# Grams of two steps in a row, then the value products of two steps in a row, in the similarity loop of a metaformer block

## The chip, the cores and the metric

The kernel runs on 1 core of one Trainium2 chip. The metric is the device time of one execution in microseconds (us); lower is better.

## What is computed

The input is x with 32 images of 64 channels and 48 x 48 pixels (P = 2304 pixels). Two blocks follow each other; the change lies in the first.

```
def _L0_conv_ref(x, Wc, bc):            # GAMMA = 2, EPS = 1e-08
    xf = x.reshape(B, C, P)
    nrm = jnp.maximum(jnp.sqrt(jnp.sum(xf * xf, axis=1)), EPS)
    xn = xf / nrm[:, None, :]
    s = jax.nn.relu(jnp.einsum('bcp,bcq->bpq', xn, xn)) ** GAMMA
    g = jnp.einsum('oc,bcp->bop', Wc, xf) + bc[None, :, None]
    out = jnp.einsum('bpq,bcq->bcp', s, g)
...
x = x + _L0_conv_ref(_ln_c(x), L0_conv_Wc, L0_conv_bc)
t = _to_tokens(x)
t = t + _L0_ffn_ref(_ln_t(t), ...)
```

So each image (the kernel calls it a batch b) needs a matrix of cosines of all 2304 x 2304 pairs of its pixels (the gram), its relu squared, and the product of that with g (the values). `_L0_ffn_ref` is a mixture of four experts whose gates come from attention over a graph of 262,144 edges between tokens.

## The kernel before, in words

The engines run programs of their own, written out by hand, and meet at semaphores. The span has four stages: images 0 to 7 together with the sorting of the edges (to about 1400 us); images 8 to 31, which is the loop of this study, from 1408 to 3683 us, while GpSimd gathers rows of the graph one after the other; the segments of the graph (to about 4350 us); the experts.

In the loop an image has STEPS = 45 steps t. The pixels of the output are cut in five chunks `CH` (four of 512 columns, one of 256, here called wide and narrow), and for each chunk the other pixels are taken in PAIRS = 9 pairs of 128 rows, so t = 9 x chunk + pair. For a step:

- PE makes a gram: for each of two row groups one matmul of high by high and low parts and one that adds the rest, both in f16 (lines 1874 and 1875), into the tile `gram[(par + t) % 2]`. There are two such tiles, used in turn; `par` changes with each image and 45 is odd, so the turns go on across images.
- ACT makes `rel`, the scaled relu of the gram (line 2064). In every third step (t % 3 == 0) ACT also squares it into `s2` (line 2068).
- In the other steps DVE multiplies the gram by `rel` into `s2` (line 2404). It reads the gram tile too, so the tile is free only after it.
- PE multiplies `s2` with the values `gT` into `acc` (function `values`, line 1830, two f32 products in the two halves of the columns, four matmul records in the trace), three steps late (LAG = 3). In the last narrow steps, and in the three first of the next image, these matmuls have 256 columns.

A gram waits for the last reader of its tile, two steps back, by one of these:

```
if t % 3 == 2:
    pe.wait_ge(a_rel, STEPS * own + (t - 1))
else:
    at_least(pe, v_s2, by_dve(STEPS) * own + by_dve(t - 1))
```

Between the steps stands work for the image before and the image after. On PE, after the values of the steps named: `post` (steps 5, 7, 9), `tokens` (15, 17), `pre` (19, 21, 23), `turn` (33, 35). On ACT, after the relu (and square) of the steps: `post` (6, 8, 10), `deviation2` (12), `tokens` (16, 18), `pre` (20, 22, 24), `deviation`, `norm`, `high` (26, 28, 30), `turned` (34, 36: copies into `hl`, line 1987). On DVE, after its product: `sums` of a finished chunk (3, 12, 21, 30, 39), norms, `value_rows` (28: `vr` line 2360 and `gT` line 2362), `units` (29), `low` (31) and, for the first sixteen of the loop's images, `level` (a piece of the graph's sorting). The function `walk` runs the body for the first image, twice in each turn of two program loops, and for the last image. After the last image SP lifts `img_done`, for which GpSimd waits before the next stage.

Of the kernel before, what the change touches and what calls it, by code (L numbers as in the profile page):

```python
# [22 lines left out]
P = 128  # L23
# [11 lines left out]
def chunks(n, size=512):  # L35
    return [(o, min(size, n - o)) for o in range(0, n, size)]
# [1201 lines left out]
def flow(nc, n, Wc, bc, Wg, att_s, att_d, b_gat, gamma, beta, W1, b1, W2, b2):  # L1238
# [5 lines left out]
    CH = chunks(NP)  # L1244
    NCH = len(CH)
    PAIRS = QT // 2
    STEPS = NCH * PAIRS
# [45 lines left out]
    with ExitStack() as ctx, ExitStack() as early, ExitStack() as late:  # L1293
# [3 lines left out]
        def sem(name):  # L1297
            return ctx.enter_context(nc.semaphore(name))

        def im_sb(name, shape, dt=F32):  # L1300
            return early.enter_context(nc.sbuf_tensor(name, shape, dt))

        def im_pb(name, shape):
            return early.enter_context(nc.psum_tensor(name, shape, F32))

        def ph(name, shape, dt=F32):
            return late.enter_context(nc.sbuf_tensor(name, shape, dt))
# [27 lines left out]
        hl = im_sb("hl", [P, 2, NP], F16)  # L1335
        lh = im_sb("lh", [P, 2, NP], F16)
# [8 lines left out]
        gram = [im_pb(f"gram{i}", [P, 2, 512]) for i in range(2)]  # L1345
# [6 lines left out]
        own = ph("own", [P, 2, TW, RW])  # L1352
# [70 lines left out]
        pe_gram = sem("pe_gram")  # L1423
        a_rel = sem("a_rel")
        a_s2 = sem("a_s2")
        v_s2 = sem("v_s2")
# [86 lines left out]
        def by_dve(k):  # L1513

            return k - (k + 2) // 3
# [5 lines left out]
        def at_least(eng, semaphore, value):  # L1521

            if not isinstance(value, int) or value > 0:
                eng.wait_ge(semaphore, value)
# [240 lines left out]
        def _(pe):  # L1765
            n.merge_tensor(pe)
            def pre(b, par, i):

                if i == 0:
                    at_least(pe, n.a_tn, NB * (b - 1))  # L1770
                else:
                    pe.wait_ge(n.a_cv, NB * b + i)
                s0, k = BATCH[i]
                for s in range(s0, s0 + k):
                    for h in range(2):
                        rows = slice(h * C, (h + 1) * C)
                        last = pe.matmul(misc[:, h, (s - s0) * P:(s - s0 + 1) * P], xh[rows, par, s * P:(s + 1) * P], n.wpre[rows, :],  # L1777
                                         start=True, stop=True)
                last.then_inc(n.pe_pre, 1)

            def turn(b, i):

                q0, k = TBATCH[i]
                if i == 0:
                    pe.wait_ge(n.v_lo, b + 1)
                if i >= 2:
                    pe.wait_ge(n.a_hl, NTB * b + i - 1)
                bank = misc[:, i % 2, :].bitcast(F16)
                for q in range(q0, q0 + k):
                    last = pe.transpose(bank[:, (q - q0) * P:(q - q0 + 1) * P], tw[:, q, :, :].rearrange("p a c -> p (a c)"), n.ident16[:, :])  # L1790
                last.then_inc(n.pe_tr, 1)

            def post(b, par, i):

                if i == 0:
                    pe.wait_ge(n.v_x2, NCH * (b + 1))
                    at_least(pe, n.a_tn, NB * b)
                else:
                    pe.wait_ge(n.a_c2, NB * b + i)
                s0, k = BATCH[i]  # L1800
                for s in range(s0, s0 + k):
                    for h in range(2):
                        rows = slice(h * C, (h + 1) * C)
                        last = pe.matmul(misc[:, h, (s - s0) * PW:(s - s0 + 1) * PW], x2[rows, par, s * P:(s + 1) * P], n.wpost[rows, :],  # L1804
                                         start=True, stop=True)
                last.then_inc(n.pe_post, 1)

            def tokens(b, i):

                if i == 0:  # L1810
                    pe.wait_ge(n.v_t2, b + 1)
                if i >= 2:
                    pe.wait_ge(n.a_tn, NB * b + i - 1)
                s0, k = BATCH[i]
                for s in range(s0, s0 + k):
                    last = pe.transpose(misc[:, i % 2, (s - s0) * P:(s - s0 + 1) * P], t2[:, s, :, :].rearrange("p a c -> p (a c)"), n.ident[:, :])
                last.then_inc(n.pe_tt, 1)

            def values(b, own, par, u):

                c, k = divmod(u, PAIRS)
                w = CH[c][1]
                pe.wait_ge(v_s2, by_dve(STEPS) * own + by_dve(u + 1))
                pe.wait_ge(a_s2, by_act(STEPS) * own + by_act(u + 1))
                if k == 0:
                    at_least(pe, n.v_x2, NCH * b + c - 1)
                    if c == 0:
                        pe.wait_ge(n.v_g, b + 1)
                for j in (0, 1):
                    last = pe.matmul(acc[(par + c) % 2][j * C:(j + 1) * C, 0:w], gT[:, par, 2 * k + j, :], s2[:, u % SLOTS, j * w:(j + 1) * w],  # L1830
                                     start=k == 0, stop=k == PAIRS - 1)
                if k == PAIRS - 1:
                    last.then_inc(n.pe_acc, 1)

            used = 0
            for turn_no, kind in enumerate(ROUTES):
# [3 lines left out]
                for q in range(banks_of(kind)):  # L1840
                    if used >= 3:
                        pe.wait_ge(a_route, used - 2)
                    bank = routed_ps[0:rows_out, used % 3, :].rearrange("p (j c) -> p j c", c=rows_in)
                    used += 1
                    for k in range(min(per, count - q * per)):
                        j = q * per + k
# [4 lines left out]
                        last = pe.transpose(bank[:, k, :], part, n.ident[:, :])  # L1851
# [7 lines left out]
                        turn(FIRST, i)  # L1859
            pe.wait_ge(a_route, routes_done[-1])  # L1860

            def body(b, own, par, nth, before, more, moved=None):
                pe.wait_ge(n.l_in[par], 32 * (nth + 1))
                for t in range(STEPS):
                    c, k = divmod(t, PAIRS)
                    o, w = CH[c]
                    if t % 3 == 2:
                        pe.wait_ge(a_rel, STEPS * own + (t - 1))
                    else:
                        at_least(pe, v_s2, by_dve(STEPS) * own + by_dve(t - 1))  # L1870
                    bank = gram[(par + t) % 2]
                    for j in (0, 1):
                        pixels = slice((2 * k + j) * P, (2 * k + j + 1) * P)
                        pe.matmul(bank[:, j, 0:w], hl[:, par, pixels], hl[:, par, o:o + w], start=True, stop=False)  # L1874
                        last = pe.matmul(bank[:, j, 0:w], lh[:, par, pixels], hl[:, par, o:o + w], start=False, stop=True)  # L1875
                    last.then_inc(pe_gram, 1)
                    if t >= LAG:
                        values(b, own, par, t - LAG)
                    elif before:
                        values(b - 1, own - 1, 1 - par, STEPS + t - LAG)  # L1880
                    if before and t in POST_PE:
                        post(b - 1, 1 - par, POST_PE[t])
                    if before and t == 15:
                        tokens(b - 1, 0)
                        tokens(b - 1, 1)
                    if before and t == 17:
                        tokens(b - 1, 2)
                    if more and t in PRE_PE:
                        if t == 19:
                            pe.wait_ge(n.x_in[1 - par], 64 * (nth + 1 + par))  # L1890
                        pre(b + 1, 1 - par, PRE_PE[t])
                    if more and t == 33:
                        turn(b + 1, 0)
                        turn(b + 1, 1)
                    if more and t == 35:
                        turn(b + 1, 2)
            walk(pe, body)
            for t in range(LAG):
                values(B - 1, NI - 1, 1, STEPS + t - LAG)
# [9 lines left out]
            for k in range(3):  # L1909
                for q in range(G):  # L1910
                    last = pe.transpose(turn_ps[:, k, q * P:(q + 1) * P], tails[:, k, q, :], n.ident[:, :])  # L1911
                last.then_inc(pe_tails, 1)
            pe.wait_ge(v_car, 1)
            for k, t in enumerate((So, Mo)):
                for q in range(G):
                    last = pe.transpose(back_ps[:, k, q, :], t[:, q * P:(q + 1) * P], n.ident[0:NC5, 0:NC5])
# [764 lines left out]
```

## Time and profile before

| | us |
|---|---|
| median of 3 runs | 5337.25 (5335.33 to 5337.66) |
| span of the profiled execution, first to last instruction | 5332.3 |
| PE busy (matmul) | 3735.5 (70%) |
| DVE busy | 3969.2 (74%) |
| ACT busy | 3397.9 (64%) |
| POOL busy | 2944.3 (55%) |

The profiled execution's own time isn't listed beside its span; the span lies 3.0 us under the fastest run and 4.9 under the median. PE is TensorE's matmul row, DVE VectorE, ACT ScalarE, POOL GpSimd, SP SyncE. In a timeline row stand the start, the duration, the engine, the line, the operation, output and inputs, the shape and how many were merged; in brackets the idle time of the engine before it and what ended it. The end of a matmul is modelled, and starts 0.22 us apart with durations of 0.38 are matmuls that follow each other without a gap. PEclk is the share of TensorE's full clock that was granted.

### The profile page before, as it was taken

How to read it: one execution, taken by the hardware profiler on the slowest of the kernel's cores; microseconds unless marked ns; L12 is line 12 of the kernel's file. 1: busy time of each engine (PE TensorE's matmuls, PEld its weight loads, DVE VectorE, ACT ScalarE, POOL GpSimd, SP SyncE). 2: the span in 40 equal slices, each digit the busy share in tenths (PEclk: the TensorE clock that was granted, in tenths of full speed). 3: DMA queues.
4: the chain of work that ended last, by engine and by line, in shares of the span. 5: the costliest groups of instructions: out<-in, count | busy, mean ns of one | idle time of the engine just before them, and what ended most of it. 6: DMA issues, size and time to landing. Idle time of an engine off the chain costs nothing.

```text
span 5332.3 us, 61957 instructions
## 1 busy us (share of the span) xinstructions
PE 3735.5 (70%) x18367; PEld 1259.1 (24%) x18367; DVE 3969.2 (74%) x5512; ACT 3397.9 (64%) x4285; POOL 2944.3 (55%) x2937
## 2 busy tenths in 40 slices
PE   4888988400599999999999999996000017787888
PEld 1223333200233333333333333332000002222222
DVE  8998988997666666666666654554999947787877
ACT  4777988401676767676676776775566536666665
POOL 6000000058777777777777777774666147666661
PEclk9899999755799999999999999998555558888889
DMA  6100100002112122222212222223555526999997
GB/s 259 33 20 25 29 20 17 15 14 82 28 41 58 40 61 48 47 58 46 62 42 52 52 46 56 42 46 87 189 184 186 184 75 137 150 160 162 158 161 141
DMA packets 332447, 441.38 MB, mean 83 GB/s; under 512 B 183193, under 2 KB 261916, under 8 KB 331500
## 3 DMA queue, kind: packets, MB, share of 16 engines
q1 hardware_dynamic: 209744, 288.12, 19.8%
q0 software_dynamic: 105536, 148.61, 16.0%
q10 hardware_dynamic: 16896, 1.18, 0.2%
q8 instruction: 152, 2.49, 0.2%
q14 instruction: 119, 0.97, 0.1%
HBM read 252.35 MB, written 166.47 MB: 79 GB/s over the span
## 4 chain that ended last, share of the span: by engine, by line
PE 36%; DVE 26%; issue 6%; ACT 5%; DMA 5%; POOL 1%; SPq 1%; DVEq 0%; ACTq 0%; POOLq 0%
PE acc L1830 13%; PE gram L1874 8%; PE gram L1875 6%; DVE s L2404 3%; DMA gs<-gates_d 3%; PE ye L1928 2%; PE up L1940 2%; ACT rel L2064 2%; DVE S L2503 2%; DVE AD L2488 2%; DVE AE L2482 2%; DVE ms L2623 1%; POOL R L1761 1%; PE misc L1804 1%; PE misc L1777 1%
## 5 line engine op out<-in xcount | busy, mean ns | idle before, releaser
L980 POOL DMA_INDIRECT rows<-htab_d,idx x2048 | 2141.5, 1046 | 730.7 <-issue 599.0
L2404 DVE SCALAR_TENSOR_TENSOR s<-gram,rel 128x1024 f32<-128x1024 f32 (+1 forms) x720 | 802.6, 1117 | 849.2 <-ACT rel L2064 844.1
L2064 ACT ACTIVATE rel<-gram 128x1024 f32<-128x1024 f32 (+1 forms) x1080 | 1009.5, 940 | 605.4 <-PE gram L1875 570.4
L1830 PE MATMUL acc<-s,gT 128*64 128x512 f32 (+1 forms) x4320 | 1076.6, 577 | 0.0
L1874 PE MATMUL gram<-hl 128*128 128x512 f16 (+1 forms) x2160 | 776.7, 365 | 117.3 <-DVE s L2404 95.9
L1875 PE MATMUL gram<-hl,lh 128*128 128x512 f16 (+1 forms) x2160 | 765.8, 360 | 0.0
L1761 POOL DMA_INDIRECT R<-seg_d,nidx x576 | 584.5, 1015 | 191.2 <-issue 165.9
L1928 PE MATMUL ye<-hid,w 128*64 128x384 f32 x1536 | 381.4, 577 | 250.8 <-DVE ms L2623 188.5
L1080 POOL IOTA slots<- 64x2048 int32 x1 | 1.8, 1832 | 974.4 <-POOLq L192 974.4
L2156 ACT ACTIVATE hid<-up,b1t 128x768 f32<-128x768 f32 x384 | 333.2, 899 | 259.6 <-PE up L1940 258.4
L1911 PE MATMUL tailsT<-ident,tails 128*20 128x128 f32 x24 | 4.7, 385 | 599.6 <-DVE tails L2511 599.6
L1874 PEld LDWEIGHTS gram<-hl 128*128 128x128 f16 x2160 | 211.0, 98 | 854.0 <-DVE s L2404 387.7
L906 ACT ACTIVATE w_s2r<-w_gram 128x1024 f32<-128x1024 f32 (+1 forms) x360 | 348.6, 968 | 93.2 <-PE w_gram L775 92.7
L316 DVE TENSOR_TENSOR edges<-edges 128x2048 f32<-128x2048 f32 (+1 forms) x186 | 370.7, 1993 | 46.9 <-ACT edges L935 41.2
L1940 PE MATMUL up<-tne,w 64*128 64x384 f32 x1536 | 403.0, 606 | 0.8 <-DVEq L2525 0.6
L317 DVE TENSOR_TENSOR edges<-edges 128x2048 f32<-128x2048 f32 (+1 forms) x186 | 369.7, 1987 | 0.0
L749 PE MATMUL w_acc<-w_s2r,w_gT 128*64 128x512 f32 (+1 forms) x1440 | 364.0, 585 | 0.6 <-ACT w_s2r L888 0.6
L888 ACT ACTIVATE w_s2r<-w_s2r 128x1024 f32<-128x1024 f32 (+1 forms) x360 | 361.5, 1004 | 0.0
L2068 ACT ACTIVATE s<-rel 128x1024 f32<-128x1024 f32 (+1 forms) x360 | 349.7, 971 | 11.4
L2623 DVE SCALAR_TENSOR_TENSOR ms<-ye,b2c,gs 128x384 f32<-128x384 f32 x384 | 232.2, 616 | 148.8 <-PE up L1940 100.9
L1830 PEld LDWEIGHTS acc<-s,gT 128*64 128x64 f32 x4320 | 214.5, 135 | 414.2 <-issue 400.8
L774 PE MATMUL w_gram<-w_hl 128*128 128x512 f16 (+1 forms) x720 | 264.6, 373 | 44.6 <-DVEq L491 13.3
(372 smaller groups left out, 5351.0 us busy)
## 6 DMA issues: line engine op xcount, KB each, us to landing
gs<-gates_d SPq DMA_DIRECT2D x64, 1024.0 KB
rows<-htab_d,idx POOLq DMA_INDIRECT x2048
seg_d<-state SPq DMA_DIRECT2D x32, 996.0 KB, 4.8
raw_d<-w_zeros POOLq DMA_DIRECT2D x48, 512.0 KB, 23.3
raw_d<-rows POOLq DMA_DIRECT2D x32, 768.0 KB, 3.7
tne<-tn_d SPq DMA_DIRECT2D x32, 576.0 KB
x2e<-x_d SPq DMA_DIRECT2D x32, 576.0 KB
out<-res SPq DMA_DIRECT2D x64, 256.0 KB
```

What stands on the lines that cost most here:

```text
L316: dve.tensor_tensor(lo, a, b, ALU.min)
L317: step(dve.tensor_tensor(hi, a, b, ALU.max))
L749: last = pe.matmul(acc[(b + c) % 2][j * C:(j + 1) * C, 0:w], gT[:, b % 2, 2 * k + j, :], s2(s)[:, j * w:(j + 1) * w], start=k == 0, stop=k ...
L980: pool.indirect_dma_start(out=n.rows[:, k % 2, j, :], out_offset=None, in_=n.htabx, in_offset=bass.IndirectOffsetOnAxis(ap=n.idx[:, g % 2, ...
L1761: pool.indirect_dma_start(out=R[:, par, j, :], out_offset=None, in_=n.seg, in_offset=bass.IndirectOffsetOnAxis(ap=nidx[:, par, j:j + 1], a ...
L1830: last = pe.matmul(acc[(par + c) % 2][j * C:(j + 1) * C, 0:w], gT[:, par, 2 * k + j, :], s2[:, u % SLOTS, j * w:(j + 1) * w], start=k == 0 ...
L1874: pe.matmul(bank[:, j, 0:w], hl[:, par, pixels], hl[:, par, o:o + w], start=True, stop=False)
L1875: last = pe.matmul(bank[:, j, 0:w], lh[:, par, pixels], hl[:, par, o:o + w], start=False, stop=True)
L1928: last = pe.matmul(y[i % 2][h * C:(h + 1) * C, 0:EW], w2[:, k, :], hid[:, i % GROUP, h, :], start=True, stop=True)
L1940: last = pe.matmul(up[i % GROUP][:, h, 0:EW], w1[rows_, k, :], tne[rows_, par, cp * EW:(cp + 1) * EW], start=True, stop=True)
L2064: act.activation(rel[:, t % RELS, 0:2 * w].rearrange("p (j x) -> p j x", j=2), gram[(par + t) % 2][:, :, 0:w], ACT.Relu, scale=1.0 / SPLIT ...
L2404: dve.scalar_tensor_tensor(halves(s2[:, t % SLOTS, 0:2 * w]), gram[(par + t) % 2][:, :, 0:w], 1.0 / SPLIT ** 2, halves(rel[:, t % RELS, 0: ...
```

## The change

The code that makes a gram becomes a function `gram_of(own, par, t)`, unchanged inside, waits included. In the loop it is called for t and t + 1 when t is even, and the values follow as before, so PE runs gram t, gram t + 1, values t - 3, values t - 2. Step 44 stays single. Programs of ACT, DVE, POOL and SP are the same.

```diff
+            def gram_of(own, par, t):
+                c, k = divmod(t, PAIRS)
+                o, w = CH[c]
+                if t % 3 == 2:
+                    pe.wait_ge(a_rel, STEPS * own + (t - 1))
+                else:
+                    at_least(pe, v_s2, by_dve(STEPS) * own + by_dve(t - 1))
+                bank = gram[(par + t) % 2]
+                for j in (0, 1):
+                    pixels = slice((2 * k + j) * P, (2 * k + j + 1) * P)
+                    pe.matmul(bank[:, j, 0:w], hl[:, par, pixels], hl[:, par, o:o + w], start=True, stop=False)
+                    last = pe.matmul(bank[:, j, 0:w], lh[:, par, pixels], hl[:, par, o:o + w], start=False, stop=True)
+                last.then_inc(pe_gram, 1)
+
             def body(b, own, par, nth, before, more, moved=None):
                 pe.wait_ge(n.l_in[par], 32 * (nth + 1))
                 for t in range(STEPS):
...
+                    if t % 2 == 0:
+                        gram_of(own, par, t)
+                        if t + 1 < STEPS:
+                            gram_of(own, par, t + 1)
                     if t >= LAG:
                         values(b, own, par, t - LAG)
                     elif before:
```

PE's order before, two steps in a wide chunk (grams 13 and 14 of an image in the first program loop; `gram0` and `gram1` are the two gram tiles, `acc0` takes the values):

```order
L1874 MATMUL gram0<-hl 128x512 [waits v_s2]
L1875 MATMUL gram0<-hl,lh 128x512
L1874 MATMUL gram0<-hl 128x512
L1875 MATMUL gram0<-hl,lh 128x512
L1830 MATMUL acc0<-s2,gT 64x512 [waits a_s2,v_s2]
L1830 MATMUL acc0<-s2,gT 64x512
L1868 REGISTER_ALU
L1874 MATMUL gram1<-hl 128x512 [waits a_rel]
L1875 MATMUL gram1<-hl,lh 128x512
L1874 MATMUL gram1<-hl 128x512
L1875 MATMUL gram1<-hl,lh 128x512
L1830 MATMUL acc0<-s2,gT 64x512 [waits a_s2,v_s2]
```

The same place in the change (grams 14 and 15, with what follows them):

```order
L1872 MATMUL gram1<-hl 128x512 [waits a_rel]
L1873 MATMUL gram1<-hl,lh 128x512
L1872 MATMUL gram1<-hl 128x512
L1873 MATMUL gram1<-hl,lh 128x512
L1524 REGISTER_ALU
L1872 MATMUL gram0<-hl 128x512 [waits v_s2]
L1873 MATMUL gram0<-hl,lh 128x512
L1872 MATMUL gram0<-hl 128x512
L1873 MATMUL gram0<-hl,lh 128x512
L1830 MATMUL acc0<-s2,gT 64x512 [waits a_s2,v_s2]
L1830 MATMUL acc0<-s2,gT 64x512
L1824 REGISTER_ALU [waits v_s2]
```

The second gram, with its wait for the tile's reader, has moved ahead of the values of both steps.

A place with work of the image before, PE's `tokens` (`misc<-ident,t2`), before:

```order
L1824 REGISTER_ALU [waits v_s2]
L1830 MATMUL acc0<-s2,gT 64x512 [waits a_s2]
L1830 MATMUL acc0<-s2,gT 64x512
L1816 MATMUL misc<-ident,t2 128x128 [waits v_t2]
L1816 MATMUL misc<-ident,t2 128x128 x7
L1524 REGISTER_ALU
L1874 MATMUL gram1<-hl 128x512 [waits v_s2]
```

And in the change:

```order
L1830 MATMUL acc0<-s2,gT 64x512 [waits a_s2,v_s2]
L1830 MATMUL acc0<-s2,gT 64x512
L1824 REGISTER_ALU [waits v_s2]
L1830 MATMUL acc0<-s2,gT 64x512 [waits a_s2]
L1830 MATMUL acc0<-s2,gT 64x512
L1816 MATMUL misc<-ident,t2 128x128 [waits v_t2]
L1816 MATMUL misc<-ident,t2 128x128 x7
L1524 REGISTER_ALU
L1872 MATMUL gram1<-hl 128x512 [waits v_s2]
L1873 MATMUL gram1<-hl,lh 128x512
```

All such work stands after the values of odd steps, which is the end of a pair, so it has kept its place and never comes between the two grams or the two values.

## Rows read from the trace of the kernel before

**Rows 1.** The page: span and busy time of each engine
```profile
span 5332.3 us, 61957 instructions
PE 3735.5 (70%) x18367; PEld 1259.1 (24%) x18367; DVE 3969.2 (74%) x5512; ACT 3397.9 (64%) x4285; POOL 2944.3 (55%) x2937
```
**Rows 2.** Windows: busy PE, PEld, DVE, ACT, POOL, then PEclk, DMA share, GB/s
```profile
1600.00:1800.00 200.00, 188.77 (x966) 61.84 (x966) 130.45 (x181) 138.40 (x194) 151.52 (x154) 0.99 0.25 58
```
**Rows 3.** Timeline (start, us, engine, line), steps 4 and 5 of image 16
```profile
2173.64 0.39 PE L1874 MATMUL gram<-hl 128*128 128x512 f16 x1
...
2174.30 0.38 PE L1875 MATMUL gram<-hl,lh 128*128 128x512 f16 x1
...
2174.61 1.08 PE L1830 MATMUL acc<-s,gT 128*64 128x512 f32 x4
2174.84 1.01 ACT L2064 ACTIVATE rel<-gram 128x1024 f32<-128x1024 f32 x1
...
2175.62 0.39 PE L1874 MATMUL gram<-hl 128*128 128x512 f16 x1
...
2175.87 1.23 DVE L2404 SCALAR_TENSOR_TENSOR s<-gram,rel 128x1024 f32<-128x1024 f32 x1 [2.02 <-ACT rel L2064]
```
**Rows 4.** Waits, 3640 to 3720 us: total, times, longest
```profile
POOL got L1716 <- SPq L1633: 53.7, 1, 53.7
```
**Rows 5.** Timeline, steps 0 to 3 of image 16
```profile
2166.17 0.39 PE L1874 MATMUL gram<-hl 128*128 128x512 f16 x1
...
2167.33 1.02 ACT L2064 ACTIVATE rel<-gram 128x1024 f32<-128x1024 f32 x1 [1.00 <-PE gram L1875]
...
2168.38 1.06 ACT L2068 ACTIVATE s<-rel 128x1024 f32<-128x1024 f32 x1
...
2169.34 2.03 ACT L2064 ACTIVATE rel<-gram 128x1024 f32<-128x1024 f32 x2
...
2170.38 2.35 DVE L2404 SCALAR_TENSOR_TENSOR s<-gram,rel 128x1024 f32<-128x1024 f32 x2 [3.00 <-ACT rel L2064]
2171.66 0.39 PE L1874 MATMUL gram<-hl 128*128 128x512 f16 x1 [0.77 <-DVE s L2404]
```
**Rows 6.** Timeline, PE at the end of the loop, narrow steps
```profile
3678.96 0.65 PE L1830 MATMUL acc<-s,gT 128*64 128x256 f32 x4
3679.55 0.28 PE L1874 MATMUL gram<-hl 128*128 128x256 f16 x1
...
3680.09 2.13 PE L1830 MATMUL acc<-s,gT 128*64 128x256 f32 x16
```
**Rows 7.** Timeline, steps 28 to 31 of image 16
```profile
2228.69 0.39 PE L1874 MATMUL gram<-hl 128*128 128x512 f16 x1 [0.35 <-DVE s L2404]
...
2232.04 1.35 DVE L2360 TENSOR_TENSOR vr<-cv,rstd 128x1152 f32<-128x1152 f32 x1
...
2234.70 1.22 DVE L2404 SCALAR_TENSOR_TENSOR s<-gram,rel 128x1024 f32<-128x1024 f32 x1
...
2235.97 0.39 PE L1874 MATMUL gram<-hl 128*128 128x512 f16 x1 [1.28 <-DVE s L2404]
```
**Rows 8.** Timeline, steps 34 to 37 of image 16
```profile
2244.00 0.38 PE L1874 MATMUL gram<-hl 128*128 128x512 f16 x1
...
2246.06 1.94 ACT L1987 ACTIVATE hl<-misc 128x1024 f16<-128x1024 f16 x2
...
2250.22 0.28 PE L1874 MATMUL gram<-hl 128*128 128x256 f16 x1 [0.55 <-DVE s L2404]
```
**Rows 9.** Timeline, the first gram of images 15, 17 and 18
```profile
2072.13 0.39 PE L1874 MATMUL gram<-hl 128*128 128x512 f16 x1 [1.86 <-DVE s L2404]
...
2262.37 0.61 PE L1874 MATMUL gram<-hl 128*128 128x512 f16 x1 [2.23 <-issue]
...
2357.52 0.39 PE L1874 MATMUL gram<-hl 128*128 128x512 f16 x1
```
**Rows 10.** Windows, the start of image 17
```profile
2262.40:2265.40 3.00, 3.00 (x9) 0.83 (x10) 0.00 (x0) 1.02 (x1) 2.09 (x4) 0.50 0.10 16
```

More of the change, by code:

```diff
@@ L1864, in body @@
                 for t in range(STEPS):
[L1865 to L1876, printed above, removed]
+                    if t % 2 == 0:
+                        gram_of(own, par, t)
+                        if t + 1 < STEPS:
+                            gram_of(own, par, t + 1)
                     if t >= LAG:
```

## The prediction

> **What bounds the kernel now.** I read the page first: over the whole span PE is busy 70%, DVE 74%, ACT 64%, so the page alone names no bound [rows 1]. The change touches one stage, the loop over 24 batches, so that stage is read by itself. In a stretch of 200 us in it PE is busy 188.77 us, ACT 138.40, DVE 130.45, at a granted clock of 0.99 [rows 2]. PE is the bound there, with some 6% of idle time, and two engines with slack behind it. Then the timeline: how does one step run? Call G(t) the four gram matmuls of step t (0 to 44), V(t) its value product, R, Q and S its relu (ACT), its square (ACT, only for t a multiple of 3) and its product on DVE (all other t). G4 starts at 2173.64 and G5 at 2175.62: a step of 1.98 us in which PE never stops [rows 3]. Last, the end of the stage: POOL waits 53.7 us for SP, which waits for the last batch [rows 4], so POOL's gathers are done before the loop is; what the loop gains or loses goes into the end of the kernel one to one.
>
> The reader should also see what ties PE to the other two. There are two gram tiles. G(t+2) writes the tile that R(t) and S(t) read. In a quiet step R starts 1.16 to 1.20 us after G, takes 1.02, S takes 1.23, and PE may go on 0.05 later: 1.16 + 1.02 + 0.03 + 1.23 + 0.05 = 3.49 us after the start of G(t) [rows 3, 5]. PE itself comes back after two steps, 3.96. The slack is 0.47 us.
>
> **Part one of the change: fewer changes between the two kinds of matmul.** Nothing is added or removed: 4 gram matmuls and 4 value matmuls a step in both orders, the same ACT, DVE and DMA work, no queue but PE's touched. What changes is how often PE goes from grams (f16, whole array) to values (f32, two halves of the columns) and back. From G4 to the first of its values: gram matmuls start (2174.30 - 2173.64) / 3 = 0.22 us apart, but the value starts 0.31 after the last of them: 0.09 for the turn [rows 3]. The way back: at the end of the stage a lone narrow V is followed by a gram after 0.59 us, but four V in a row take 2.13 against 0.65 for one, (2.13 - 0.65) / 3 = 0.49 each: again 0.09 to 0.10 [rows 6]. Each pair of steps loses one turn each way, 0.18 us, and there are 22 pairs in 45 steps: 22 x 0.18 = 3.96 us less PE work a batch, 95 us in 24 batches. That is the whole gain, and it is a gain only where PE sets the pace. The Trainium skill says of this (TensorEngine Tiling (Array Packing), Key Properties) that changing the tiling mode drains the engine; by that rule alone the change would be a pure win of the size just given.
>
> **Part two: the second gram of a pair is late.** A quiet pair now takes 2 x 1.98 - 0.18 = 3.78 us, and its second gram starts 0.88 after the first (4 x 0.22). So G(t+3) is due 3.78 + 0.88 = 4.66 us after G(t), t even, and needs the tile that R(t+1) and S(t+1) read. ACT and DVE now get both grams close together and work them off one after the other. Three cases:
> - No other work between: R ends at 2.18, the second R at 3.20, two S from 2.21 take 2.35 together [rows 5], ready at 4.56 + 0.05 = 4.61. Due 4.66. It fits, with nothing to spare, where there was 0.47.
> - t a multiple of 6: Q(t) stands in ACT's queue between R(t) and R(t+1). The trace already has this chain, at the start of a batch, where the steps are short: R0, Q0, R1, S1, and G3 starts 2171.66 - 2166.17 = 5.49 us after G0 [rows 5]. Its members follow each other without a gap, so it doesn't depend on when G1 came. PE stands 5.49 - 4.66 = 0.83 us. Before, Q cost nothing: G(t+1) came 1.98 after G(t), and its R would have had to start at 3.14, when ACT is free at about 3.2.
> - DVE or ACT have a longer piece between the pair's two readers: below.
>
> The values V(t-3) and V(t-2) are queued behind the waiting gram on PE, though what they need is long ready; DVE's additions of a finished chunk wait for those, but V follows within 2 us, when DVE is still busy with S. No second-order wait is counted.
>
> **The sum for one batch**, extra standing time against before:
> - G3. The values before it are narrow (0.49): due 4 x 0.22 x 3 + 2 x 0.49 + 0.18 = 3.80, ready 5.49, stands 1.69 where it now shows 0.77: +0.9 [rows 5].
> - Pairs at t = 6, 12, 18, 24, one Q each: 4 x 0.83 = +3.3.
> - G31. DVE makes vr and gT between S28 and S29. From G28 to G31 are 2235.97 - 2228.69 = 7.28 us; due after 4.66: stands 2.62, now 1.28: +1.3 [rows 7].
> - G37. ACT copies hl (1.94) between R34 and R35. G34 to G37 are 2250.22 - 2244.00 = 6.22; due after 3.78 + 0.13 (two turning matmuls) + 0.45 (narrow gram) = 4.36: stands 1.86, now 0.55: +1.3 [rows 8].
>
> Together +6.8 us, less 3.96 saved: **+2.8 us a batch**. The Q pair at t = 30 falls in the shadow of G31, the narrow ones at 36 and 42 find short readers: nothing. Over 24 batches 67 us, less 2 for the last, which has neither vr nor hl: +65. The sum stands against the profiled span: 5332.3 + 65 = 5397; the median of the runs lies 5 us above that span (5337.25), so 5402. The clock adds about 2 (next part): 5404, +1.25%.
>
> What I could not read: a pair's waits in the loop. Below, the four Q stalls may partly coincide with standing time that the batch has already (the second group of post matmuls waits for ACT at t = 7, G27 for DVE): if half of them do, 1.7 us a batch less, 5404 - 40 = 5364, and if turns save more than 0.09 each this goes on. Above, other pieces of ACT (at t = 8, 10, 16, 20, 22) also stand between a pair's two relus; the longest shown is hl's 1.94, which behind PE's own extra matmuls of about 1.1 us leaves 1.94 - 0.05 - 1.1 = 0.8, and two such a batch give +38: 5442. I take the middle since the four Q places are nearest to the chain of rows 5, which is measured whole.
>
> **The rivals.**
> 1. Faster. The turn is saved and the second gram isn't late, because its tile comes free within 4.66 us of G(t). Then PE paces the loop as now and time falls by up to 95: 5242. For it: PE is the engine at 94%, ACT and DVE are a third idle [rows 2], and the quiet chain of 4.61 does fit. Against: wherever Q stands between, the trace has 5.49, and a saving of 0.18 a pair cannot pay 0.83 in every third pair. It decides at a stall of 0.54 for each Q if nothing else got worse. Chance 0.07.
> 2. Nothing that can be told (within 0.2%, about what a measurement of this kernel can tell from no change): only part of each comes. Chance 0.04.
> 3. The clock falls. After a wait of 2.23 us at a turn of the program loop PE was granted 0.50, that is 1.2 GHz instead of 2.4, and matmuls of 0.39 took 0.61 [rows 9, 10]. That batch took 2357.52 - 2262.37 = 95.15 us with the clock low at its start; one where it stayed up took 94.04: a fall costs 1.1. G31 will stand 2.6 us in every batch, G3 and G37 nearly 2. If each batch falls once at full price: + 26, 5430; twice: 5456. Against: behind G31, PE is ahead of ACT and DVE anyway and stands again at G33, so slow matmuls there cost little; hence only 2 us in the forecast. The Trainium skill (TensorE: Matmul & The Clock Gate, A second HAM failure mode: psum-queue depth-cycling) tells of just such small idle times between groups of matmuls making the clock swing; by that page this rival would be the likelier. Chance 0.13.
> 4. The turns are not saved in the loop, since a V behind a V has waits with values from registers, which the rows of the stage's end lack. PE would lose 22 x 0.18 a batch, but a third of pairs wait for ACT or DVE anyway: + 30 to 60, 5434 to 5464. Chance 0.05.
>
> **How the numbers follow.** Forecast 0.71, rival 1 0.07, rival 2 0.04, rivals 3 and 4 0.18; I give 0.01 of the first more to faster for what I misread. Predicted 5404. The range runs from 5375, some 30 below by coinciding stalls, to 5445, which takes in the ACT pieces and a clock fall in most batches; rival 1, the far ends of 3 and 4 and the lowest bound stay out, some 0.2. Faster 0.08, same 0.04, slower 0.88.
>
> **What would show it.** In the profile after: eight gram matmuls and then eight value matmuls in a row, with no gap between the two values; PE busy in the loop down from 188.8 to about 175 of 200 (idle 5.3 + 6.8 of 97 us a batch); a stall of 0.8 before the second gram of the pair after each Q, released by DVE; 2.6 at G31, 1.7 at G3; batches of about 97 us instead of 94.0; POOL's wait for SP up from 54 to about 120. I am wrong if G(t+3) follows G(t) by less than 5.3 where Q(t) lies between, or if batches take under 94.

## The result and the profile after

| | before | the change |
|---|---|---|
| median of the runs, us | 5336.29 (4 runs) | 5374.47 (4 runs, 5371.23 to 5379.01) |
| ratio to before | | 1.0071, 95% interval 1.0056 to 1.0085 |
| span of the profiled execution | 5332.3 | 5369.4 |

The change makes the kernel 38 us slower, 0.71%: a small difference, but the interval excludes none at all. The forecast was 5404 with a range from 5375 to 5445. The direction is right, the size is not, and the result lies just under the range.

The page and the window of the loop that answer to [rows 1, 2]:

```profile
span 5369.4 us, 61957 instructions
...
PE 3662.2 (68%) x18367; PEld 1334.2 (25%) x18367; DVE 3966.2 (74%) x5512; ACT 3387.0 (63%) x4285; POOL 2943.6 (55%) x2937
```
```profile
1600.00:1800.00 200.00, 178.86 (x940) 66.78 (x937) 128.44 (x179) 136.33 (x193) 152.33 (x157) 0.97 0.23 52
```

PE is busy 178.86 of 200 us instead of 188.77, with the same matmuls to do: it turns between the two kinds less often and waits more. From the first gram of the loop to the last are 2313.2 us, before 2272.0: 41 us, which is all of the 38 us and 3 more. The wait of POOL for the loop's end [rows 4] has grown as said, but from 53.7 to 101.4 and not to 120:

```profile
POOL got L1716 <- SPq L1633: 101.4, 1, 101.4
```

Now a quiet pair, the timeline of steps 10 and 11 of image 16 (line 1872 is the gram, as 1874 before):

```profile
2203.89 0.39 PE L1872 MATMUL gram<-hl 128*128 128x512 f16 x1
...
2205.41 0.38 PE L1873 MATMUL gram<-hl,lh 128*128 128x512 f16 x1
...
2205.72 1.94 PE L1830 MATMUL acc<-s,gT 128*64 128x512 f32 x8
...
2207.59 0.39 PE L1872 MATMUL gram<-hl 128*128 128x512 f16 x1
```

Two wide values in a row are one group of 1.94 us where one took 1.08 [rows 3], so the second adds 0.86; the pair takes 2207.59 - 2203.89 = 3.70 us, not 3.78. (A bracket counts from the modelled end of the matmul before it. In front of a second gram it therefore shows 0.38 - 0.22 = 0.16 us less than the gram is late.) And the three places where the second gram was to wait. The start of image 16, against [rows 5]:

```profile
2181.26 0.39 PE L1872 MATMUL gram<-hl 128*128 128x512 f16 x1
...
2183.47 1.06 ACT L2074 ACTIVATE s<-rel 128x1024 f32<-128x1024 f32 x1
...
2184.43 1.92 ACT L2070 ACTIVATE rel<-gram 128x1024 f32<-128x1024 f32 x2
...
2185.47 2.36 DVE L2410 SCALAR_TENSOR_TENSOR s<-gram,rel 128x1024 f32<-128x1024 f32 x2 [3.06 <-ACT rel L2070]
2186.75 0.39 PE L1872 MATMUL gram<-hl 128*128 128x512 f16 x1 [1.50 <-DVE s L2410]
```

G0 to G3: 5.49 us, as before, though G1 now starts 0.6 us earlier; the bracket has grown from 0.77 to 1.50. Steps 28 to 32, against [rows 7], and the granted clock behind G31:

```profile
2244.28 0.39 PE L1872 MATMUL gram<-hl 128*128 128x512 f16 x1
...
2250.29 1.22 DVE L2410 SCALAR_TENSOR_TENSOR s<-gram,rel 128x1024 f32<-128x1024 f32 x1
...
2251.56 0.61 PE L1872 MATMUL gram<-hl 128*128 128x512 f16 x1 [2.54 <-DVE s L2410]
...
2253.38 2.68 PE L1830 MATMUL acc<-s,gT 128*64 128x512 f32 x8
...
2255.99 0.39 PE L1872 MATMUL gram<-hl 128*128 128x512 f16 x1
```
```profile
2251.60:2254.60 3.00, 3.00 (x8) 0.92 (x10) 2.87 (x5) 1.29 (x2) 2.39 (x3) 0.50 0.08 8
```

G28 to G31: 7.28 us, the same again, and PE stands 2.54 us before G31 where it stood 1.28. Behind it the clock is 0.50 (1.2 GHz) for 3.4 us: matmuls of 0.39 take 0.61 and two values 2.68 instead of 1.94. Such a fall follows in each of the 23 images that have this wait (all but the last). Then G34 to G37, against [rows 8], is 2266.82 - 2260.59 = 6.23 us (before 6.22):

```profile
2260.59 0.38 PE L1872 MATMUL gram<-hl 128*128 128x512 f16 x1
...
2266.82 0.28 PE L1872 MATMUL gram<-hl 128*128 128x256 f16 x1 [1.82 <-DVE s L2410]
```

The second grams of other pairs wait too. Here are G15, which answers to a square (t = 12), and G19, where ACT makes `tf` for the image before (line 2017) between the relus of steps 16 and 17:

```profile
2213.28 0.39 PE L1872 MATMUL gram<-hl 128*128 128x512 f16 x1 [0.60 <-DVE s L2410]
...
2219.11 1.08 ACT L2017 ACTIVATE tf<-misc 128x512 f32<-128x512 f32 x2
2220.06 1.05 ACT L2070 ACTIVATE rel<-gram 128x1024 f32<-128x1024 f32 x1
...
2222.42 0.39 PE L1872 MATMUL gram<-hl 128*128 128x512 f16 x1 [0.49 <-DVE s L2410]
```

All brackets before grams that wait, in us, medians over the 22 images between the first and the last (smaller ones left out):

| gram | 3 | 9 | 13 | 15 | 19 | 21 | 25 | 27 | 28 | 31 | 33 | 37 |
|---|---|---|---|---|---|---|---|---|---|---|---|---|
| before | 0.77 | 0 | 0 | 0 | 0 | 0 | 0 | 0.05 | 0.34 | 1.28 | 1.12 | 0.55 |
| the change | 1.50 | 0.08 | 0.17 | 0.60 | 0.49 | 0 | 0.72 | 0.42 | 0 | 2.55 | 0 | 1.82 |
| q_behind (below) | 0.48 | 0 | 0.21 | 0 | 0.49 | 0 | 0.72 | 0 | 0 | 2.54 | 0 | 1.82 |

For the sum, the start of G(t) after G0 in us, medians over the same images, from the timelines of gram records, with some of the runs below:

| t | 3 | 6 | 12 | 18 | 24 | 30 | 36 | 42 | loop in all |
|---|---|---|---|---|---|---|---|---|---|
| before | 5.49 | 12.49 | 26.42 | 39.67 | 54.13 | 66.53 | 81.95 | 90.59 | 2272.0 |
| the change | 5.49 | 12.66 | 26.34 | 39.64 | 54.13 | 66.72 | 83.20 | 92.55 | 2313.2 |
| q_behind | 4.48 | 11.65 | 24.24 | 36.94 | 51.43 | 63.42 | 79.89 | 89.25 | 2244.2 |
| q_before | 5.05 | 12.05 | 25.37 | 38.39 | 52.86 | 64.73 | 80.17 | 88.81 | 2234.2 |
| split_30 | 5.50 | 12.66 | 26.34 | 39.64 | 54.13 | 66.72 | 83.01 | 92.36 | 2313.6 |
| pair_4 | 5.49 | 12.23 | 25.91 | 38.89 | 53.16 | 65.31 | 80.76 | 89.53 | 2243.0 |
| q_later | 4.48 | 11.65 | 24.24 | 36.94 | 51.43 | 63.42 | 77.32 | 85.82 | 2155.5 |

### The profile page after: what moved, and what is told of

Read it like the earlier page. It is cut to its first block, busy times and chain, and to the rows that moved or that the text cites. A ratio compares the mean times of both kernels' runs of the same rounds, so it can differ in the third digit from the quotient of the medians.

```text
span 5369.4 us, 61957 instructions
## 1 busy us (share of the span) xinstructions
PE 3662.2 (68%) x18367; PEld 1334.2 (25%) x18367; DVE 3966.2 (74%) x5512; ACT 3387.0 (63%) x4285; POOL 2943.6 (55%) x2937
## 4 chain that ended last, share of the span: by engine, by line
PE 32%; DVE 26%; ACT 9%; issue 5%; DMA 5%; POOL 1%; SPq 1%; ACTq 0%; DVEq 0%; POOLq 0%
PE acc L1830 11%; PE gram L1872 7%; PE gram L1873 6%; ACT rel L2070 5%; DVE s L2410 5%; DMA gs<-gates_d 3%; PE ye L1934 2%; DVE S L2509 2%; PE up L1946 2%; DVE AD L2494 2%; DVE AE L2488 2%; DVE ms L2629 1%; POOL R L1761 1%; PE misc L1777 1%; DMA gates_d<-GH 1%
## 5 line engine op out<-in xcount | busy, mean ns | idle before, releaser
L1830 PE MATMUL acc<-s,gT 128*64 128x512 f32 (+1 forms) x4320 | 986.7, 578 | 0.0
L1830 PEld LDWEIGHTS acc<-s,gT 128*64 128x64 f32 x4320 | 267.3, 139 | 492.9 <-issue 477.6
```

## The experiments

The kernel before took 5342 to 5351 us (medians) beside the experiments and 5336 beside the change, so ratios are compared, not times.

### Two theories of the slowdown: late tiles, or the clock

The 23 falls, at 1.61 us each (G31 to G32 takes 2255.99 - 2251.56 = 4.43 us; the same stretch of the quiet pair takes 3.70 - 0.88 = 2.82), are 37 us. That is the slowdown itself. The two theories give the same number for the change, so runs had to separate them. The first moves ACT's square out from between the two relus of a pair:

```diff
-                    if t % 3 == 0:
-                        act.wait_ge(a_rel, STEPS * own + t + 1)
-                        act.activation(s2[:, t % SLOTS, 0:2 * w], ...
+                    if t % 6 == 3:
+                        square_of(own, t)
+                    if t % 6 == 1:
+                        square_of(own, t - 1)
```

> The change, but ACT squares step t (t a multiple of 6) only after the relu of step t + 1, so that nothing stands between the two relus of such a pair. Theory A (the tile's readers come late: relu, square, relu, product, 5.5 us from G(t) to G(t+3) at every multiple of 6): the chain shrinks by the square to about 4.6, G0 to G3 falls from 5.50 to about 4.6, and each batch loses some 3 us: about 5374 - 75 = 5300, below the kernel before. Theory B (the clock is the cost: it falls to 0.50 once per batch behind G31, and 22 falls of 1.7 us are the whole 38 us): G31 stands as long as ever, the falls stay, 5374 within 10 us.

Measured: ratio 0.9946 (0.9929 to 0.9962), against 1.0071 for the change: 1.25% or 67 us less, and below the kernel before. The timeline at the start of image 16:

```profile
2156.63 0.39 PE L1872 MATMUL gram<-hl 128*128 128x512 f16 x1
...
2157.79 2.01 ACT L2075 ACTIVATE rel<-gram 128x1024 f32<-128x1024 f32 x2 [0.96 <-PE gram L1873]
...
2159.69 1.05 ACT L2065 ACTIVATE s<-rel 128x1024 f32<-128x1024 f32 x1
...
2161.11 0.39 PE L1872 MATMUL gram<-hl 128*128 128x512 f16 x1 [0.48 <-DVE s L2416]
```

The relus stand together, the square behind them, and G0 to G3 is 4.48 us, one square less. In the table of brackets the waits before G9, G15 and G27 are gone and the one before G3 is 1.0 us shorter. The loop has as many falls of the clock as the change (33 against 30 records, behind its first few steps) and is 69 us shorter. That tiles came late because of the square is shown; the clock can't be the cause of what vanished here. The second run leaves the squares and takes away the falls:

```diff
-                    if t % 2 == 0:
+                    if t in (30, 31):
+                        gram_of(own, par, t)
+                    elif t % 2 == 0:
```

> The change, but steps 30 and 31 are not paired: gram 30, values 27, gram 31, values 28. PE stands before G31 some 1.6 us instead of 2.7 and values stand between. Theory B (clock): the falls at step 31 vanish and with them 22 x 1.66 = 37 us: about 5337. Theory A: G28 to G31 stays at 7.28 us since DVE's vr and gT set it, what the clock took at step 31 was taken out of the wait before G33 anyway, and one turn more is paid: 5374 to 5398, even if the clock no longer falls.

Measured: ratio 1.0083 (1.0066 to 1.01), which can't be told from the change's 1.0071. The wait before G31 is shorter and the clock stays up:

```profile
2250.88 0.39 PE L1872 MATMUL gram<-hl 128*128 128x512 f16 x1 [1.54 <-DVE s L2412]
```
```profile
2251.00:2254.00 3.00, 2.90 (x12) 0.70 (x10) 2.87 (x4) 1.36 (x2) 2.39 (x3) 1.00 0.09 8
```

No image has a fall at step 31 any more (11 are left in the loop, 9 of them at image starts), and the loop takes 2313.6 us against 2313.2. The clock theory falls: what the slow matmuls took was free time before G33, which waits for the chain units, high, relu 31 on DVE and ACT. With the clock up, PE stands there; in the change G33 follows G32 without a wait:

```profile
2256.03 0.39 PE L1872 MATMUL gram<-hl 128*128 128x512 f16 x1 [2.13 <-DVE s L2412]
```

From G31 to G33 are 5.35 us in the change and 5.15 here, so a fall costs 0.2 us an image, 5 us in all. (The run pays one turn more an image as well, 0.26 x 24 = 6 us, so by it alone the falls cost at most some 7 us, not 37.) The third run moves that chain's head, DVE's vr and gT, behind the product of step 29:

```diff
-                    if more and t == 28:
+                    if more and t == 29:
                         value_rows(b + 1, 1 - par)
```

> The change, but DVE makes vr and gT after the product of step 29 instead of between those of 28 and 29. G31 then no longer waits for them (G28 to G31 from 7.28 to about 4.7), but units, high and the relu of step 31 behind it in DVE's and ACT's queues come later by one product, 1.2 us, and hold G33. Theory A: the wait moves from G31 to G33 and grows: no gain, 5374 to 5410. Theory C (G31 alone is what the pairing lost, its 1.3 us a batch): 5374 - 31 = 5343.

Measured: ratio 1.0161 (1.0144 to 1.0178), 0.9% more than the change, some 48 us, more than the 36 that I had allowed. G31 comes 2.7 us earlier in the image and G34 2.2 us later (81.61 after G0, in the change 79.39). PE now stands 3.93 us before G33 (median). The wait moved down the chain and grew, so G31 was not the place that counted; theory C falls.

The control, the squares moved in the kernel with single grams (same edit as the first):

> The kernel before with the same move of ACT's squares (those of t a multiple of 6 after the relu of t + 1), as control for the first run. Theory A: in the single order the square is nearly hidden (0.47 us of slack, the square costs 0.06 of it), save at G3 (stands 0.8, its chain shrinks by one square, 0.8) and in part at G28 and the post matmuls: -1 us a batch at most, 5312 to 5336, so most of what the first run gains is specific to the pairs.

Measured: ratio 0.994 (0.9924 to 0.9957), 32 us less than before, 8 more than I had allowed. In the table G3 comes 0.44 earlier and G12 - G6 falls from 13.93 to 13.32 us: in that stretch the square of step 6 stands ahead of ACT's copies that PE's post matmuls wait for, which I hadn't counted; PE's 21 waits before them (11.4 us between 1500 and 3500 us) are gone in this run. Of the 67 us that the move gained in pairs, 32 are thus to be had without pairs, and 35 belong to the pairs, nearly the whole 38 us, to within the intervals. With the squares between, pairing costs 0.7%; with the squares behind, the times don't show a cost (0.9946 against 0.9940, intervals overlap), though the loop is still 10 us longer (2244.2 against 2234.2).

### Which pairs gain

The second gram of a pair at t = 4, 10, ... takes the tile of a step that only the relu reads. Only these pairs are made here:

```diff
-                    if t % 2 == 0:
+                    if t % 6 == 4:
                         gram_of(own, par, t)
-                        if t + 1 < STEPS:
-                            gram_of(own, par, t + 1)
+                        gram_of(own, par, t + 1)
+                    elif t % 6 != 5:
+                        gram_of(own, par, t)
```

> The kernel before, with only the pairs at t = 4, 10, 16, 22, 28, 34, 40 made (7 of 22). The second gram of such a pair (t = 5, 11, ...) takes the tile of a step that is a multiple of 3, which only the relu reads, so it is free after 2.2 us and nothing has to be late. Theory A (a pair costs when its second gram waits for relu, square, relu and product, and gains its turns where it doesn't): the 7 pairs gain 0.26 us each except the two at 28 and 34, where DVE and ACT set the time anyway: 24 x 5 x 0.26 = 31 us less than the kernel before, at least 15, at most 44. Theory D (any early second gram costs by crowding ACT and DVE): a third of the 38 us, 13 us more than before.

Measured: ratio 0.9946 (0.9927 to 0.9965), 29 us less, and the loop 29 us shorter; 31 was expected. In the table the five stretches from G0 to G30, each with one such pair, are 0.19 to 0.27 us shorter than before; from G30 to G42, where DVE's and ACT's chains set the time, nothing is gained (0.16 lost). That is the price of two turns measured by itself. Its pair at t = 4 runs through without a wait, with eight values in one group:

```profile
2165.06 0.39 PE L1872 MATMUL gram<-hl 128*128 128x512 f16 x1
...
2166.89 1.94 PE L1830 MATMUL acc<-s,gT 128*64 128x512 f32 x8
```

So an early second gram is no cost in itself (theory D falls); it is one where its tile is late.

### The best order, and what bounds it

The moved squares together with the chain of steps 28 to 38 taken apart (for all pairs, for single grams, and for the pairs at t = 4, 10, ...):

```diff
-                    if more and t == 30:
+                    if more and t == 32:
                         high(b + 1)
...
-                    if more and t == 28:
+                    if more and t == 29:
                         value_rows(b + 1, 1 - par)
-                    if more and t == 29:
+                    if more and t == 31:
                         units(b + 1)
```

and low from 31 to 33, turn on PE from 33 and 35 to 35 and 37, turned on ACT from 34 and 36 to 36 and 38.

> All pairs, squares behind the second relu, and the chain vr/gT, units, high, low, turn, turned taken apart: vr and gT after the product of 29, units at 31, high at 32, low at 33, turning at 35 and 37 on PE, 36 and 38 on ACT. Theory A: the waits at G31 and G33 shrink with the one at every square, G28 to G31 falls from 7.3 to about 4.7, the clock stays up behind step 31; each batch loses 6 us against the change, 150 us: about 2% below the kernel before (ratio 0.98). Theory B would count the falls: 22 x 1.7 = 37 us less than the run with the squares alone, ratio 0.988.

> The same moves of squares, vr/gT, units, high, low and turning with single grams, as in the kernel before. It says what pairing is worth once its waits are gone: theory A has 0.6 us a batch, 14 us, in favour of the pairs (ratio 0.984 here against 0.981 there), since with both orders DVE and ACT still set part of the steps; if PE alone set the pace the pairs would be ahead by 22 x 0.26 x 24 = 137 us.

> The same moves, but pairs only at t = 4, 10, 16, 22, 28, 34, 40. Theory A: the other 15 pairs hold their second gram close to the end of the readers' chain and gain little or nothing, these 7 are free: a further 1 us a batch below all pairs, 25 us, ratio about 0.977. If every pair gained its turns, this one would be slower than all pairs by 15 x 0.26 x 24 = 94 us.

Measured: ratios 0.9857 (0.9836 to 0.9878), 0.9872 (0.9851 to 0.9894) and 0.9866 (0.9847 to 0.9885); 5270.7, 5273.9 and 5270.7 us beside 5342.1. All three gained less than expected (0.98, 0.984 and 0.977). These are the fastest versions of the study, and I can't tell them apart. Their loops are 2155.5, 2205.2 and 2153.9 us. The pairs win 50 us of loop over single grams, more than three times the 14 expected, but nothing of it arrives. And the seven pairs at t = 4, 10, ... do as much for the loop as all 22: the other 15 gain nothing here and cost nothing, where I had expected all pairs to be 25 us behind. The waits after the loop in q_later show one of 50.1 us that was 1.6 us in the kernel before (columns: total, times, longest):

```profile
DVE AE L2494 <- ACT AE L2120: 50.1, 2, 46.3
```

ACT there waits for rows that POOL fetches, and POOL no longer waits for SP at all: with a loop 116 us shorter, its gathers end after the loop. The first fetch of the next stage (line 1718) starts at 3636.7 us in q_later and at 3634.0 in q_later_before, though the loop of the one ends 49 us before that of the other:

```profile
L1718 POOL DMA_INDIRECT nb<-htab_d,node x32: 940/947/1677, 3636.7 to 4188.2; - x32
```
```profile
L1718 POOL DMA_INDIRECT nb<-htab_d,node x32: 940/947/3278, 3634.0 to 4188.5; - x32
```

So the end of the gathers, not of the loop, starts that stage in both. To see what the gathers cost, 64 or 128 of POOL's 1856 early gathers were put behind the loop's end:

```diff
-    AHEAD = 29
+    AHEAD = 28
```

> q_later, but POOL makes 28 instead of 29 groups of 64 gathers before it waits for the last image (AHEAD = 28); the 64 go into the next stage, where POOL has idle time. In q_later the loop ended 116 us earlier but the kernel only 71 us, and DVE stood 46 us for rows that POOL fetches: if POOL's gathers (64 x 1.25 = 80 us) are what the rest of the gain was lost to, this gives back about 46 us: 5225, ratio 0.977 to 0.980. If it was something else, ratio 0.986 as before; if the next stage can't take the gathers, worse than that.

> The same with 27 groups. POOL then waits for the loop by some 75 us again, so nothing more is to be had at the loop's end; 128 gathers in the next stage are 160 us there. Equal to AHEAD = 28 if that stage has the room, slower by some tens of us if not.

> q_later_4 with 28 groups. Its loop took 2154 us against 2156 of q_later: the same time as that run within 0.2%.

> q_later_before (single grams) with 28 groups. Its loop took 2205 us, 50 us more than q_later's, and POOL hid that in the former pair of runs. With POOL out of the way the two orders must differ by about these 50 us: some 5265 to 5275 here, ratio 0.986, and pairs ahead by 0.8 to 0.9%. If pairs still don't win, the loop's length is not what counts at its end.

Measured: 0.9919 (0.9901 to 0.9937), 1.0068 (1.0052 to 1.0085), 0.9918 (0.9901 to 0.9934) and 1.0004 (0.9993 to 1.0016). The hoped-for 0.978 didn't come: POOL waits for the loop again, but the next stage can't take the gathers. In q_later_a28 and then in q_later_a27:

```profile
POOL got L1716 <- SPq L1633: 27.6, 1, 27.6
...
DVE AE L2494 <- ACT AE L2120: 74.5, 3, 40.1
```
```profile
DVE AE L2494 <- ACT AE L2120: 154.9, 3, 120.7
...
POOL got L1716 <- SPq L1633: 111.3, 1, 111.3
```

DVE's wait goes from 50.1 to 74.5 and 154.9 us, and the second group costs 1.5% or 80 us, its 64 gathers at 1.25 us. The last run came out at 1.0004 and not at the expected 0.986, since the gathers cost it too, but the last two did what they were for: with POOL waiting for the loop's end in both orders (27.6 us in q_later_a28, 78.6 with single grams), pairs (0.9919) lead single grams (1.0004) by 0.85%, 45 us, as the loops say (2156.5 against 2199.3 us), and the seven pairs (0.9918) do as well as all 22. So pairing is worth its turns where no tile is late. In the versions with 29 groups POOL's gathers stand in the way of more than about 70 us of gain. That all of q_later's missing 45 us is POOL's is likely by these waits, but not shown; a run with fewer or faster gathers, which would show it, was not made.

## Why the prediction was wrong

**Right, point by point.** PE bounded the loop, and what the loop lost came out at the end (41 us of loop, 38 us of time). The three chains are what they were to 0.01 us: 5.49, 7.28 and 6.23 us. The second gram of a pair waits for the readers of its tile, and the square between the relus is one reason (q_behind). The clock falls once in an image behind G31, as rival 3 had it, and costs next to nothing, as the forecast had it (0.2 us an image): the rule of the Trainium skill (TensorE: Matmul & The Clock Gate, A second HAM failure mode: psum-queue depth-cycling) on small idle times between groups of matmuls named a real effect, but here the falls stand in time that PE would else have waited. Rival 4 (turns not saved in the loop) is refuted by the group of 1.94 us.

**The steps that failed** are in the sum for one batch, "+2.8 us"; measured +1.7 (41 us / 24). Divided at the same places (medians, the last row from means, so the rows don't add up exactly):

| stretch | forecast, stalls less turns | measured |
|---|---|---|
| G0 to G6 | 0.9 - 3 x 0.18 = +0.36 | +0.17 |
| G6 to G30 | 3.3 - 12 x 0.18 = +1.1 | +0.02 |
| G30 to G36 | 1.3 - 3 x 0.18 = +0.8 | +1.06 |
| G36 to the next image | 1.3 - 4 x 0.18 = +0.6 | +0.6 |

- "Each pair of steps loses one turn each way, 0.18 us" was too small: 3.96 - 3.70 = 0.26. This is the term that made the forecast miss. The way back from values to grams was read from narrow matmuls [rows 6], where it is 0.10; behind wide ones the second value adds 0.86 where a lone one takes 1.01 until the next gram starts (2174.61 to 2175.62, [rows 3]), so it is 0.15. The 18 pairs from t = 4 to t = 38 have a wide value there. They give back 18 x 0.08 = 1.4 us more an image, 35 us over the loop. The forecast for the loop was +65 and +41 was measured; the stalls, 0.4 us an image larger than forecast when the slow matmuls behind G31 are counted in, take back about 10. pair_4 measures the same price by itself, 0.19 to 0.27 us for a pair.
- "Pairs at t = 6, 12, 18, 24, one Q each: 4 x 0.83" has nearly the right sum in the wrong places, and that is luck. From G6 to G30 the stalls grew by 0.02 + 12 x 0.26 = 3.1 us against 3.3. But the grams G9, G15, G21 and G27 of those four pairs show brackets of 0.08, 0.60, 0 and 0.42. G9 and G21 are hardly late, because PE's own post and pre matmuls in these steps, with what they wait for, put off their due time: from G6 to G9 are 6.75 us and from G18 to G21 6.32, both longer than the chain of 5.49. The rest is G13, G19 and G25 (0.17, 0.49, 0.72), behind pieces of ACT's post, tokens and pre that stand between the relus of steps 10 and 11, 16 and 17, 22 and 23. The forecast had these at nothing in its sum and named them only for its upper bound. They are also the waits that q_behind leaves.
- From G30 to G36 the change lost 0.3 us more than forecast. "No second-order wait is counted" was the step, as far as the traces show (no run changes it alone): G33 still comes only when the chain on DVE and ACT lets it, 5.35 us after G31 (before 5.14, and 5.15 in split_30 without the fall), and behind it now stand two values instead of one, so G33 to G34 takes 3.73 us instead of 2.88. In split_30, without the fall, G33 to G34 is 3.74 as well.
- Rival 1 was nearer than it looked. With 0.26 for the two turns of a pair, a stretch of six steps pays for a stall of 0.78, not of 0.54, and from G6 to G30 the stalls grew by 3.1 / 4 = 0.78 a stretch: nothing was lost there. All of the loss lies before G6 and behind G30.

## What to carry to other kernels

Grouping work of one kind on an engine saves its turns only while each buffer's last reader still comes in time: before grouping, write down the chain from the first producer of the group to the release of the second buffer, with everything that stands in the readers' queues between the two, and compare it with the new due time. If it is late, move the odd work behind the pair or group only the steps whose buffer has a short reader (seven such pairs did as much here as all 22). Remember that what is queued behind the waiting member of the group waits with it. And take a price from rows of the same shape as the place where it will be paid, even when the other shape is the only one that stands back to back in the trace.

## What was not expected of the hardware

- From f32 values in two column halves back to f16 grams costs PE 0.15 us behind matmuls of 512 columns and 0.10 behind 256; the other way it is 0.09 for both (0.31 against 0.22 from start to start, 0.20 against 0.11 when narrow). Both ways together are 0.26 us for a pair of wide steps, measured whole.
- TensorE's clock fell to 0.50 behind a wait of 2.54 us in every image but the last, and never behind the waits of 1.54 in the same place (split_30); behind that run's waits of 2.13 before G33 it fell in 2 of 23 images. The 23 falls of 3.4 us cost the loop about 5 us and not 23 x 1.61 = 37: without them PE stands 2.13 us before G33, with them not at all.
